# Attention and feed-forward block on one core: output projection of the first eight token tiles inside the last two attention halves, attention values split where they are made, first normalisation on ScalarE

## What is computed

```python
q, k, v = (split_heads(lora_linear(x, W, b, B, A)) for W, b, B, A in qkv)   # 16 heads of 32
attn = softmax(q @ k.T * 32 ** -0.5) @ v                                    # joined to 512 columns
x1 = layernorm(x + lora_linear(attn, Wo, bo, Bo, Ao))
xt = x1.reshape(2048, 512)
e = argmax(xt @ Wg); gate = softmax(xt @ Wg)[e]        # 8 experts, 256 places each, later tokens dropped
moe = gate * (silu(xd @ W1[e]) * (xd @ W3[e])) @ W2[e] # hidden width 704
shared = silu(xt @ sw1) * (xt @ sw3) @ sw2
out = layernorm(x1 + moe + shared)
```

## Time and profile before

| | us |
|---|---|
| median of 3 runs | 1122.74 (1121.78 to 1123.65) |
| the profiled execution, its own time | 1124.97 |
| its span, from the first to the last instruction | 1123.3 |
| start of half 0 | 125.8 |
| half 13, half 14, half 15 with its end | 32.4, 26.8, 26.0 |
| from there to the first matmul of the shared expert, at 717.56 | 84.1 |
| from there to the end | 405.7 |

### The profile page before, as it was taken

The page is one execution under the profiler, slowest core; times in us unless marked ns, Lnnn a source line. Parts: engine busy times, 40 slices in busy tenths (PEclk is TensorE's granted clock), DMA queues, the critical chain, the costliest instruction groups (busy, mean ns, idle before and its releaser), DMA issues.

```text
span 1123.3 us, 16277 instructions
## 1 busy us (share of the span) xinstructions
PE 1064.0 (95%) x5710; PEld 738.1 (66%) x5710; DVE 725.5 (65%) x1202; ACT 552.1 (49%) x969; POOL 472.9 (42%) x269
## 2 busy tenths in 40 slices
PE   4899999999999999999999969899999999999995
PEld 3777556465564645555443557678899999998884
DVE  3337967878777787877775478453376666664163
ACT  4220465656566565656657422342356655663125
POOL 2100476884848678484867632047000000003500
PEclk9899999999999999999999989899999999999997
DMA  8556341402423142232356243043357677775604
GB/s 271 198 177 188 101 115 39 95 29 63 116 60 93 39 95 65 58 85 57 95 136 194 83 142 113 19 163 85 85 171 237 211 227 230 222 209 119 93 1 150
DMA packets 154533, 138.40 MB, mean 123 GB/s; under 512 B 43537, under 2 KB 119569, under 8 KB 154208
## 3 DMA queue, kind: packets, MB, share of 16 engines
q1 hardware_dynamic: 147808, 121.58, 38.7%
q0 software_dynamic: 6656, 15.93, 5.1%
HBM read 81.56 MB, written 31.47 MB: 101 GB/s over the span
## 4 chain that ended last, share of the span: by engine, by line
PE 80%; DVE 9%; ACT 3%; DMA 3%; issue 2%; SPq 2%; POOL 0%; ACTq 0%; DVEq 0%
PE bank L751 20%; PE bank L897 12%; PE bank L910 11%; PE bank L845 10%; PE bank L1028 10%; PE bank L833 8%; PE bank L922 4%; PE bank L806 3%; DVE mx L1483 2%; PE bank L758 1%; DMA raw<-in_L_ffn_W_dram 1%; DVE xTlo L1420 1%; DMA at_in<-attn_d 1%; ACT rows L1387 1%; PE bank L784 1%
## 5 line engine op out<-in xcount | busy, mean ns | idle before, releaser
L1483 DVE TENSOR_REDUCE mx<-bank 128x1 f32<-128x512 f32 x512 | 323.5, 680 | 99.1 <-PE bank L845 96.9
L1245 ACT ACTIVATE prob<-bank 128x512 f32<-128x512 f32 x512 | 289.6, 597 | 192.9 <-PE bank L897 179.6
L678 POOL TENSOR_TENSOR psum<-psum,prob 128x1024 f32<-128x1024 f32 x122 | 286.9, 2392 | 0.0
L897 PE MATMUL bank<-Qs,Ks 97*128 97x512 f32 x512 | 208.2, 423 | 1.9 <-DMA Qs<-mrow 0.9
L845 PE MATMUL bank<-Ks,Qs 96*128 96x512 f32 x512 | 188.4, 407 | 2.6 <-DVE mx L1483 1.3
L897 PEld LDWEIGHTS bank<-Qs,Ks 97*128 97x128 f32 x512 | 95.4, 188 | 112.6 <-ACT prob L1245 74.0
L678 POOL TENSOR_TENSOR psum<-prob,prob 128x1024 f32<-128x1024 f32 x32 | 75.8, 2388 | 139.0 <-PE bank L922 135.3
L910 PE MATMUL bank<-prob,V 128*32 128x512 f32 x1024 | 132.6, 606 | 0.0
L845 PEld LDWEIGHTS bank<-Ks,Qs 96*128 96x128 f32 x512 | 96.4, 189 | 44.5 <-DVE mx L1483 13.9
L730 POOL DMA_DIRECT2D oe_d<-oe_sb x16 | 8.8, 548 | 231.4 <-ACT oe_sb L1367 230.4
L833 PE MATMUL bank<-xThi,Wsl 128*128 128x512 f32 x256 | 98.0, 398 | 1.2 <-DVE plane_klo L1473 0.8
(11 more groups left out here) (222 smaller groups left out, 2111.9 us busy)
## 6 DMA issues: line engine op xcount, KB each, us to landing
raw<-in_L_ffn_W_dram SPq DMA_DIRECT2D x120, 256.0 KB, 3.6
Ks<-plane_khi SPq DMA_DIRECT2D x64, 128.0 KB, 2.3
Qs<-plane_qhi SPq DMA_DIRECT2D x64, 128.0 KB, 2.3
raw<-in_L_ffn_sw_dram SPq DMA_DIRECT2D x30, 256.0 KB, 3.6
xin<-in_L_attn_x_dram SPq DMA_DIRECT2D x16, 256.0 KB, 5.3
v_d<-v_sb POOLq DMA_DIRECT2D x16, 256.0 KB, 3.3
Wsl<-wt_d SPq DMA_DIRECT2D x16, 256.0 KB, 4.0
Ks<-plane_klo SPq DMA_DIRECT2D x32, 128.0 KB, 2.3
```

The lines of the kernel that those rows point to most:

```text
L678: po.tensor_tensor(psum[:, pr], (prob[0] if kc == 1 else psum)[:, pr], prob[kc % RING][:, pr], ALU.add).then_inc(sem("sum_done"), 1)
L897: nc.tensor.matmul(score_at(v, i), Ks[v.b][0:97, hh, kc * P:(kc + 1) * P], Qs[v.b][0:97, hh, v.hf * HALF:(v.hf + 1) * HALF], start=True, s ...
L1245: ACTV(prob[kc % RING][:, hh, :], score_at(v, i), ACT.Exp, scale=SCALE).then_inc(sem("exp_done"), 1)
L1483: ins = RED(mx[(hf + ahead) % 2][:, 4 * hh + qt, part:part + 1], src, AX.X, ALU.max)
```

## The change

- In half 14 PE projects token tiles 0 to 3 and in half 15 tiles 4 to 7, by letters `p` in the words of these halves, into the one bank that the q and k projections used (`pj`). DVE adds each to x right behind (`q` there, `tile`), so that the bank comes free. SP loads the weights, x and the attention tiles for this during halves 13 to 15.
- The attention values are split where they are made: DVE multiplies into PSUM (`n`), ACT makes the hi part (`h`, `split_hi`), DVE the lo part (`z`, `split_lo`), and SP stores both; tiles are loaded as hi and lo and go to PE as they are. `at_done`, and with it the next use of the bank of the sums, now comes after `z`. `at_hi` and `at_rest` are gone.
- The normalisation of the 16 tiles is an ACT instruction with scale and bias, where it was a DVE one. Tiles 0 to 7 are normalised together.
- All words are written anew. `SUMS` is 6 for every half. The last group moves two `m` from half 13 to half 14. POOL's bias additions for tiles 0 to 7 stand between its sums of halves 14 and 15. The 4 MB of zeros for `xd_d` are written in four parts behind halves 2, 4, 6 and 8, where one DMA wrote them behind half 13. Turned tiles use three banks, before two.

```diff
-EVEN = ("mmlvl mm pm m pm m mp mo "
-        "mmqp m e m mm mi vmm i "
-        "v m iv mm r v m mm "
-        "mi v mn mm vm - v mm")
+EVEN = ("mm vl m mm pmp mmp m p mmmq o "
+        "le i mm v im mm v mm m v "
+        "- immr vi mn v mmm - v m hmm "
+        "vm zmm")
+ODD = ("mvll mm m m m me mom m pp im "
+       "mpm - ip mm mq vvivivm mm npp p mqp "
+       "mvh zm rp - mmp m mmp m mm vv "
+       "- mpmq")
...
+LAST_EVEN = ("mmlv mm m l mo mm em im mvm p "
+             "mi mp m mqp pm im mpi q p ppmvv "
+             "mm p qn pr pq - p vv ph pp "
+             "p vvz")
+LAST_ODD = ("ii q - ilv o - - - - lep "
+            "- pip - - pvvv - p qp n p "
+            "p - vhv p zppp - - q q ppp "
+            "- plvve")
-SUMS = [6] * (HALVES - 2) + [5, 4]
+SUMS = [6] * (HALVES - 3) + [6, 6, 6]
@@ SP
+            if v.last and v.slot == 1:
+                load_wo()
             if v.last and v.slot == 2:
-                load_wo(v)
+                load_bo(v)
+                load_at(0)
+            if v.last and v.slot == 3:
+                load_at(1)
+                load_xr(1)
...
+        def load_at(i):
+            sp.wait_ge(sem(f"at_st{i % 2}"), 32 * (2 * NG + i // 2))
+            for t in range(4 * i, 4 * i + 4):
+                if t >= 4:
+                    sp.wait_ge(sem("o_full"), t - 3)
+                for s in range(2):
+                    sp.dma_start(f32(at[t % 4][s][:]), attn_cols[s][:, :, t * P:(t + 1) * P]).then_inc(sem(f"at_ld{t % 4}"), 16)
@@ PE
+        def project(t, quarters=range(DC)):
+            if 0 in quarters:
+                pe.wait_ge(sem(f"at_ld{t % 4}"), t // 4 * 32 + 32)
...
+                elif t < NT // 2:
+                    pe.wait_ge(sem("y_done"), t)
@@ PE, after the last half
-        for i in range(4):
-            project(i)
-            if i >= 2:
-                logits(i - 2)
-            if i:
-                turn_x1(i - 1)
-        turn_x1(3)
+        for t in range(8, 12):
+            project(t)
+        turn_x1(0, 4)
+        for t in (12, 13):
+            project(t)
+        turn_x1(4, 8)
+        logits(0)
+        for t in (14, 15):
+            project(t)
+        logits(1)
+        turn_x1(8, NT)
@@ ACT
+        def split_hi(v):
+            ac.wait_ge(sem("norm_done"), v.n)
+            if v.n >= 2:
+                ac.wait_ge(sem(f"at_st{v.hf}"), 32 * (v.n // 2 + 1))
+            ACTV(attn_hi[:], dn, ACT.Identity).then_inc(sem("attn_hi"), 1)
...
         def end(v):
-            at_hi(0)
-            at_hi(1)
+            root(1, 0, 8)
             take_ov(v)
+            x1(1, 0, 5)
+            split_hi(v)
+            x1(1, 5, 8)
@@ DVE
-            TT(attn_sb[hf][:], attn_sb[hf][:], dn, ALU.mult).then_inc(sem("at_done"), 1)
+            TT(dn, attn_sb[hf][:], dn, ALU.mult).then_inc(sem("norm_done"), 1)
+        def split_lo(v):
+            ve.wait_ge(sem("attn_hi"), v.n)
+            TT(attn_sb[1 - v.hf][:].bitcast(FR), dn, f32(attn_hi[:]), ALU.subtract).then_inc(sem("at_done"), 1)
...
         def end(v):
-            at_rest(0)
-            at_rest(1)
+            variances(0, 8)
+            scales(1, 0, 8)
             invert(v, 0, 4)
             norm_out(v)
+            split_lo(v)
@@ POOL
+                if n >= HALVES - 2:
+                    for t in RESIDUAL_BEHIND[n - HALVES][kc]:
+                        residual(t)
```

More of the change, by code:

```diff
@@ L131, in half_order @@
 def half_order(slot, last):
-    if last and slot >= 2:
-        text = LAST_ODD if slot == 3 else LAST_EVEN
+    if last and slot:
+        text = (LAST_FIRST, LAST_EVEN, LAST_ODD)[slot - 1]
     else:
@@ L144, in half_uses @@
     odd = slot % 2
-    uses = smax_uses(1, EARLY[odd]) + ([] if last and slot >= 2 else smax_uses(2, 0, EARLY[1 - odd]))
+    if last and slot:
+        uses = smax_uses(1, EARLY[1]) + smax_uses(2, 0, LAST_EARLY) if slot == 1 else smax_uses(1, LAST_EARLY)
+    else:
+        uses = smax_uses(1, EARLY[odd]) + smax_uses(2, 0, EARLY[1 - odd])
     order = []
@@ L330, in emit @@
     wide = Arena(nc, overlay, sum_at)
-    rows = wide("rows", [P, NT, D], F32)
+    rows_b = wide("rows_b", [P, NT // 2, D], F32)
+    w13 = [[wide(f"w13_{c}{s}", [P, 2, DC, P], FR) for s in ("hi", "lo")] for c in range(2)]
     late = Arena(nc, sum_at, nc.sbuf_usable_end)
@@ L356, in f32, with rows @@
         return ap.bitcast(F32)
+    def rows(t):
+        return (rows_a if t < NT // 2 else rows_b)[:, t % (NT // 2)]
     def w_bank(k):
@@ L965, in half @@
                         piece += 1
+                    elif w == "p" and v.last and v.slot >= 2:
+                        project(4 * (v.slot - 2) + piece // DC, (piece % DC,))
+                        piece += 1
                     elif w in "mr":
@@ L1248, in half @@
                             take_ov(v)
+                        elif w == "h" and not v.first:
+                            split_hi(v)
                         elif w == "q" and v.proj:
@@ L1279, in _, with x1_hi @@
         ACTV(wgp[0][:, :, 0:E], wg_raw[:], ACT.Identity).then_inc(sem("wgp_hi"), 1)
-        def x1_hi(i):
-            for j in range(4):
-                turned(i, j, x1_bank(4 * i + j), ("x1_t", 0), "x1_hi")
+        def x1_hi(start, stop):
+            for t in range(start, stop):
+                turned(t // 4, t % 4, x1_bank(t), ("x1_t", 0), "x1_hi")
         def take_logits(i):
@@ L1528, in half @@
                         norm_out(v)
+                    elif w == "z" and not v.first:
+                        split_lo(v)
+                    elif w == "q" and v.last and v.slot >= 2:
+                        tile(4 * (v.slot - 2) + done)
+                        done += 1
         def invert(v, start, stop):
@@ L1616, in step @@
                ALU.subtract).then_inc(sem("hid_lo"), 1)
-        link = Chain(ve, sem("ln1_chain"))
-        for i in range(4):
-            tiles(i, link)
-            variances(link, "ln1")
-            if i:
-                x1_rest(i - 1)
-            scales(link, i + 1, "ln1")
-            for j in range(4):
-                t = 4 * i + j
-                TS(rows[:, t], rows[:, t], mv[:, j, 0:1], ln_r[:, j:j + 1], ALU.subtract, ALU.mult).then_inc(sem("x1_rdy"), 1)
-            if i in FIRST_PROJ:
-                conv(13, FIRST_PROJ[i], 0)
-        x1_rest(3)
+        for t in range(8, 12):
+            tile(t)
+        variances(8, 12)
+        x1_rest(0, 4)
+        scales(2, 8, 12)
+        for t in (12, 13):
+            tile(t)
+        x1_rest(4, 8)
+        conv(13, 0, 0)
+        for t in (14, 15):
+            tile(t)
+        variances(12, NT)
+        scales(3, 12, NT)
+        x1_rest(8, 12)
+        conv(13, 1, 0)
+        x1_rest(12, NT)
+        conv(13, 2, 0)
         step(0, 0, 512)
@@ L1703, in add_shared @@
                     ve.wait_ge(sem(f"all_added{t}"), 16)
-                TT(rows[:, t], bank[4 + j], rows[:, t], ALU.add).then_inc(sem("acc_done"), 1)
+                TT(rows(t), bank[4 + j], rows(t), ALU.add).then_inc(sem("acc_done"), 1)
         for c in range(FC):
@@ L1759, in _ @@
             if c == 3:
-                scales2(1, 0, 12)
+                scales2(4, 0, 12)
         for t in range(12, NT):
```

297 lines of the change are left out of this document (156 added, 141 removed), and 9 rows, old and new, of tables (LAST_EVEN, LAST_ODD, ODD).

## The result

The changed kernel takes 1130.07 us, the median of 7 runs from 1126.83 to 1131.78; the kernel before, run beside it, 1121.19 (7 runs, 1118.12 to 1123.65). The ratio is 1.0078 with a 95% interval from 1.0059 to 1.0096: slower by 0.8%, where 1105 was forecast. The profiled execution took 1128.98, and its span, 1127.4, stands against 1123.3 before.

The account below looks back on a forecast made before the run. PE was taken to set the steady halves, with a hole in the token-tile stage after attention. Terms 0 - 3.0 + 9.1 + 13.4 - 37.5 = -18.0 us gave 1105 us; forecast 1100 to 1110 (chance 0.56), range 1096 to 1118.

Parts of the forecast that it names:

- The zeros: Halves 0 to 12: parts of the 4 MB of zeros, in a DMA queue a third busy, cost nothing.
- the lower bound: Halves 0 to 12: the split costs nothing; upper bound 0.69 in each of 13 halves, +9.0; +2.0 taken.
- The -2.0 for one group fewer: Halves 0 to 12: odd word has 5 groups instead of 6; six pairs at 0.34 us give -2.0 us.
- Half 13: Two `m` fewer, evenly placed: 29.4 us where it took 32.4, so -3.0 (bounds -4.6 and 0).
- Half 14: Added projection matmuls: 35.9 us, before 26.8, +9.1; no wait for attention tiles (bounds 0 and +2).
- Half 15: With its end: 33.2 us of work plus two waits of 3.1, 39.4, before 26.0; +13.4 (bounds +9 and +18).
- the wait for x: Half 15: 1.2 us for x within POOL's chain of sums and bias additions, done at 36.6.
- The wait for the first tile: Half 15: first `p` at 6.4 us, its tile lands at about 9.5, so PE waits 3.1.
- D to `up(0)`: End of half 15 (D) to the shared expert's first matmuls: 46.6 us, before 84.1, -37.5 (bounds 41 and 56 us).
- The four normalisations: Behind tile 15, before `up(0)`: four on ACT take 2.4 us on the path, 0.5 us more than on DVE.
- a split that stops PE in every half: Rival, halves 0 to 12: late `z` fills `m` banks and PE waits, 1.7 a half, +22, 1127; chance 0.05.
- The loads' round trips cost more: Rival: first tile 4 us later in halves 14, 15 and behind half 15; waits grow about 10, 1115; chance 0.17.

Follow-up runs that it names:

- the second store: Kernel before, each half's values written twice, the second copy to a tensor nothing reads; 1125.98 us, ratio 1.0036.
- the early load: Changed kernel with the next group's q and k weights loaded in halves 4 and 8, ahead of store and zeros; 1116.32 us, ratio 0.9957.
- the old words with the split: Changed kernel with the early load and the kernel before's steady step order, only `h` and `z` put in; 1112.66 us, ratio 0.9913.
- x first: Changed kernel with the early load and x of tiles 12 to 15 loaded between the attention tiles, not behind them; 1111.70 us, ratio 0.9901.
- zeros late: Changed kernel with the four parts of the zeros behind halves 10 to 13; ratio 1.0031.
- zeros elsewhere: Changed kernel with the four parts of the zeros behind halves 2, 6, 10 and 12; 1128.06 us, ratio 1.0065.
- zeros in the kernel before: Kernel before with the zeros in four parts behind halves 2, 4, 6 and 8; 1130.87 us, ratio 1.0093.

## Why the prediction was wrong

Point by point, each by the step of the prediction.

*The zeros, the step that failed.* "The parts of the 4 MB of zeros lie in a DMA queue that is a third busy in this stage: nothing." The share of a third was read from a window of 445 us. Half 5's first 14.5 us had 0.61 before, and there stood a load that PE waited for already. What it should have asked is what is queued behind each new DMA on SP, and which engine waits for that. What the runs showed in its place: a part of 1 MB ahead of the weight load of halves 5 and 9 makes these halves 3.1 and 6.9 us longer than a steady one in the kernel before, and adds 5.0 in the two together on top of the second store. With the zeros alone the kernel before loses 0.93%, more than the whole of the result (0.78%).

*The doubled store, left out of the sum.* The split of the values was costed as one instruction of DVE and one of ACT, and its second DMA of 256 KB only in halves 14 and 15. In halves 5 and 9 it stands ahead of the same weight load: 6.3 us there in the kernel before (0.36% of the whole), 9.2 in the changed one. Store and zeros together are 13.6 of the 17.1 us by which halves 0 to 12 grew, and the early load takes 14.1 off these halves.

*Halves 0 to 12 otherwise.* The split hides wholly, as the lower bound had it: the old words with the split run at the old speed. The waits of PE in the steady pair of the kernel after (us in total, times, longest) say the same; its wait for DVE is 1.3, and was 0.8:

```profile
PEld bank L943 <- ACT prob L1308: 9.7, 21, 0.8
...
PEld bank L891 <- DVE mx L1557: 1.3, 3, 0.8
```

The -2.0 for one group fewer was wrong in sign: +3.4. I had the price of a group from one place of the trace and did not ask what the new order does to other waits. The first of these two rows is 1.6 us longer than before (8.1), so PE's pace in these halves may have more in it than the count of matmuls and groups. Which step of the words it is stays open.

*Half 13*: -3.7, -3.0 expected. *Half 14*: 36.7, expected 35.9; PE waited for no attention tile, as said.

*Half 15*: 42.9 where 39.4 was expected. The chain is the one named, POOL's sums. POOL began 6.7 us into the half (6.5 expected) but was done at 38.5 (36.6): the wait for x took 3.2 and not 1.2. From there to D it is 4.5 where 2.8 was counted. The wait for the first tile (3.1 in the sum, 1.6 measured) hides in front of POOL's.

*D to `up(0)`*: 47.9, expected 46.6. The sum was near, in part by luck, since its chain was another: POOL waited 17.7 us for x of the last tiles, and the load of tile 12 is not on the chain. The four normalisations took 2.92 and not 2.4. With x first the stage takes 45.1 to 45.5. The move of the normalisation cost what its direction promised: from start to start one takes 0.48 us on DVE and 0.73 on ACT with scale and bias (8 in 5.9, below), so the four on the path cost 1.0 us more than on DVE, 0.5 more than was counted; the prediction had taken a plain copy's 0.6. The rule of the Trainium skill that the prediction weighed ("VectorE: DVE Perf Modes", the perf-mode tier table), `tensor_scalar` in fp32 at twice the rate of `tensor_tensor`, points the same way; the trace agrees as to DVE, 0.48 beside 0.69.

```profile
L1341 ACT ACTIVATE rows_a<-rows_a,ln_shift,ln_scale 128x512 f32<-128x512 f32 x8 | 5.9, 804 | 0.0
```

*The rivals.* None had the place. The one that ended near the time, 1127 by a split that stops PE in every half, was near by luck: its cause is not there, as the old words with the split show. "The loads' round trips cost more" had the right kind of cause, stores and loads that stand ahead of a load in one queue, but looked at the last halves alone. What the forecast took for the likeliest case, 1105, is what the kernel does when the two costs of the queue, the new words, some of POOL's additions and the late x are taken away (ratio 0.9858). It stands near the forecast's terms stage by stage, half 15 at 40.9 for 39.4 and D to `up(0)` at 45.1 for 46.6, but it is another kernel than the one forecast.

## What to carry to other kernels

A DMA that is added to a queue is costed by what stands behind it there within the next few microseconds and by who waits for that; a queue that is a third busy over a stage can be full where the stage's one urgent load stands. Look for a wait on a DMA in the trace of before, however short: 0.4 us of it says that this load has no slack. When such a load is found, moving it ahead of the bulk can be worth more than making the bulk smaller (here 14 us, where moving the zeros away gave some 5), and when a change costs time in an unexpected stage, a table of the loop's passes finds it at once: two of thirteen took 7 us more.

## What the runs showed of the hardware

An issue of a DMA on SP can be held while much is in the queue: two issues took 1.35 us before, 6.94 behind 1 MB of zeros, 9.79 behind 2 MB. And a load of 0.5 KB, whose own issue was not held, landed 4.28 us later before, 5.99 behind a second store in the kernel before, 7.16 behind it in the changed kernel without the zeros near.

The zeros' packets are small: in 22 us around them the trace of after counts 4704 packets under 512 bytes, that of before 576. 1 MB landed 8.6 us behind its issue, 2 MB 12.1, so the second MB took 3.5 us, about 300 GB/s (an estimate from the two). The Trainium skill ("DMA: Bandwidth & Descriptors", Specifications) says that a transfer needs 512 bytes or more for line rate and that a smaller one becomes a read, modify and write. No run here shows it: none wrote the same bytes in larger packets, so whether that would have cost less is open.

A wait of PE in these halves mostly cost more than itself, because the granted clock fell to 0.50 (1.2 GHz) for some microseconds. A wait of 3.0 us cost 4.8 (the second store), 3.4 cost 5.3 and 2.1 cost 3.9 (zeros late, halves 5 and 9), 3.6 cost 6.0 and 1.9 cost 3.8 (zeros elsewhere), 5.4 cost 7.3 (the changed kernel). But a wait of 2.9 in half 5 (zeros in the kernel before) cost 3.1 and one of 1.2 (the second store, half 9) cost 1.5, and the clock stayed at 1.00. A wait of 1.9 was followed by the low clock and one of 2.9 was not: its length alone does not tell.
